# A vision tower's setup: which engine finishes the last parameters, and where the second pictures are waited for

## The reference, cut to what matters

```
y    = relu(batchnorm(conv1_w @ x + conv1_b))          # 64 -> 16 channels
wdyn = conv2_w @ y + conv2_b                           # 9 weights for each place
h    = sum over the 9 taps of shifted(x) * wdyn        # per picture, 64 channels
h    = concat(cls_tok, h)                              # 4 x 4097 x 64
```

```
Lr, Li, Delta = -exp(log_real), imag, exp(log_Delta)
Lbar  = exp(Lr*Delta) * (cos(Li*Delta), sin(Li*Delta))
denom = max(Lr*Lr + Li*Li, 1e-12)
inv_L = (Lr/denom, -Li/denom)
coeff = inv_L * (Lbar - 1)                             # complex product
B_bar = coeff * (B_real, B_imag)
h = h + y_forward + flip(y_backward)      # scan with Lbar, B_bar in, C out, then gelu
```

## Time and profile before

| | us |
|---|---|
| median of three runs | 637.13 |
| lowest and highest of them | 635.39, 638.50 |
| the profiled execution, whole | 637.52 |
| its span, first to last instruction | 636.0 |
| setup, from the span's start to PE's first matmul of the involution | 19.74 |
| involution, from there to PE's first matmul of the next stage | 121.3 |
| PE busy | 567.5 (89%) |
| DVE busy | 504.2 (79%) |
| POOL busy | 423.6 (67%) |
| ACT busy | 291.2 (46%) |

### The profile page before, as it was taken

How to read it: one execution, slowest core, us unless ns; L and a number is a source line. 1 busy time by engine, 2 the same in 40 slices (tenths; PEclk the granted TensorE clock), 3 DMA queues, 4 the chain that set the end, 5 groups by cost and what they waited for, 6 DMA issues and landing times. The chain is left out here.

```text
span 636.0 us, 9633 instructions
## 1 busy us (share of the span) xinstructions
PE 567.5 (89%) x2964; PEld 430.6 (68%) x2964; DVE 504.2 (79%) x919; ACT 291.2 (46%) x822; POOL 423.6 (67%) x641
## 2 busy tenths in 40 slices
PE   0699999985565799999998999999999999999993
PEld 0387878875453688788886667777777777767672
DVE  6688898866663678878789388888888888988885
ACT  3123322225443112235567466766666777655410
POOL 1688999934553033346756178888888888897776
PEclk9999999999785899999999899999999999999998
DMA  6200000000000000000000000000000000000001
GB/s 257 63 3 0 1 2 1 0 0 2 1 1 1 0 1 1 0 1 1 2 1 0 1 1 18 18 17 18 17 19 18 16 18 18 7 11 17 18 18 33
DMA packets 13144, 9.83 MB, mean 15 GB/s; under 512 B 4524, under 2 KB 12844, under 8 KB 12844
## 3 DMA queue, kind: packets, MB, share of 16 engines
q1 hardware_dynamic: 13084, 9.29, 4.6%
q10 hardware_dynamic: 16, 0.00, 0.0%
HBM read 5.10 MB, written 4.20 MB: 15 GB/s over the span
## 5 line engine op out<-in xcount | busy, mean ns | idle before, releaser
L1578 PE MATMUL ex_pE<-ex_WdP,ex_hid 128*128 128x512 f32 (+1 forms) x516 | 183.8, 407 | 0.0
L1578 PEld LDWEIGHTS ex_pE<-ex_WdP,ex_hid 128*128 128x128 f32 (+1 forms) x516 | 96.5, 187 | 32.4 <-issue 11.0
L1821 POOL TENSOR_TENSOR ex_s<-ex_ms 128x1024 f32<-128x1024 f32 (+1 forms) x33 | 83.0, 2514 | 47.4 <-DVE ex_ms L1699 47.2
L1699 DVE TENSOR_TENSOR ex_ms<-ex_pE,ex_gate 128x512 f32<-128x512 f32 x129 | 87.6, 682 | 29.1 <-PE ex_pE L1578 29.0
L1578 PE MATMUL ex_pE<-WdL,ex_hid 128*128 128x512 f32 x258 | 101.7, 394 | 0.0
L816 DVE TENSOR_TENSOR inv_prod<-inv_pW,m_img 128x504 f32<-128x504 f32 x144 | 89.2, 679 | 14.1 <-PE inv_pW L731 13.5
L746 PE MATMUL inv_pS<-ident,inv_prod 128*128 128x128 f32 x576 | 87.3, 275 | 0.7 <-ACT hT L781 0.7
L746 PEld LDWEIGHTS inv_pS<-ident,inv_prod 128*128 128x128 f32 x576 | 71.4, 142 | 16.7 <-DVE inv_prod L816 7.4
L1445 POOL TENSOR_TENSOR hT<-hT,m_M 128x512 f32<-128x512 f32 x24 | 34.0, 1430 | 67.6 <-ACT m_M L1395 67.6
L731 PE MATMUL inv_pW<-inv_ysb,m_conv2L 98*128 98x512 f32 x144 | 75.3, 526 | 2.9 <-DVE inv_ysb L804 2.3
L279 DVE TENSOR_TENSOR ex_hid<-ex_hidf,ex_hid 128x512 fp32r<-128x512 f32 (+1 forms) x64 | 61.1, 973 | 0.0
(11 more groups left out here) (248 smaller groups left out, 1130.7 us busy)
## 6 DMA issues: line engine op xcount, KB each, us to landing
m_img<-in_x SPq DMA_DIRECT2D x2, 2048.0 KB, 9.1
out<-ex_res SPq DMA_DIRECT2D x16, 256.0 KB, 2.3
WdT<-in_L_ffn_Wd SPq DMA_DIRECT2D x2, 256.0 KB
bd<-in_L_ffn_bd SPq DMA_DIRECT2D x16, 2.0 KB
W1d<-in_L_ffn_W SPq DMA_DIRECT2D x2, 64.0 KB
m_Bm<-in_L_attn_fwd_B_real SPq DMA_DIRECT2D x2, 16.0 KB, 1.9
m_Bm<-in_L_attn_fwd_B_imag SPq DMA_DIRECT2D x2, 16.0 KB, 2.1
m_Bm<-in_L_attn_bwd_B_real SPq DMA_DIRECT2D x2, 16.0 KB, 2.0
```

What stands on the lines that cost most here:

```text
L1578: last = nc.tensor.matmul(pE[n % 3][0:P].rearrange("p e f -> p (e f)"), hid[i % 2][value][:, h, par, 128 * j:128 * j + P], WdP[weight][:, ...
L1699: nc.vector.tensor_tensor(ms[b % NB][0:P, t % TPB, :].rearrange("p (e f) -> p e f", e=EX), pE[n % 3][0:P], gate[i % 2][0:P, t, :].unsqueez ...
L1821: nc.gpsimd.tensor_tensor(s4[0:P, 0:T], m[:, :, 0:4 * F], m[:, :, 4 * F:], ALU.add).then_inc(halved, 1)
```

## The change

Five edits, all in the first two stages.

1. DVE's list in setup now ends with the reciprocal (`1/denom`). The fifteen steps on `S` and `decay` that followed leave it.
2. They are written, as sixteen steps, at the head of `state_matrices`, so GpSimd does them at the start of its list in the involution. (One fused step becomes two: a product and a change of sign.) Five of the sixteen are issued without a wait for their own end.
3. The two copies of C (`Cin`, 64 x 64 each) go to GpSimd's list in setup, behind a wait for C's four transfers. PE's transposes of C wait for these copies.
4. The four slices of `m.N` go to ScalarE's list in setup, as activations (`Copy` with a scale), behind a wait for PE's transposes.
5. SP's wait at the end of setup is for the first pictures only. The second pictures have a semaphore of their own, `second_in`, and PE and VectorE wait for it in the involution before they first read them.

The diff, without the lines that only declare a semaphore:

```diff
@@ setup, DVE
                 link(vec.reciprocal(s(15), s(14)))
-                tt(s(16), s(13), s(15), ALU.mult)
-                stt(s(17), imag, -1.0, s(15), ALU.mult, ALU.mult)
-
-                v.wait_ge(c_in, 16 * 4)
-                for d in range(2):
-                    copy(Cin[:, d, 2, :], Cin[:, d, 0, :])
-                count("c_laid")
-                v.wait_ge(exped, 3)
-                v.wait_ge(sined, 3)
-                tt(s(10), s(9), s(9), ALU.mult)
...
-                tt(g.decay[:], s(21), s(21), ALU.mult)
-                v.wait_ge(c_turned, 1)
-                for d in range(2):
-                    ts(m.N[:, 0, d, slot_n(d, 0), :], pC[:, 2 * d, :], sgn[:, 0:1], None, ALU.mult)
-                    ts(m.N[:, 1, d, slot_n(d, 0), :], pC[:, 2 * d + 1, :], -1.0, None, ALU.mult)
@@ setup, SP
-                image(1)
-                sp.wait_ge(img_in, 32)
+                image(1, m.second_in)
+                sp.wait_ge(img_in, 16)
@@ setup, GpSimd
+                pool.wait_ge(c_in, 16 * 4)
+                for d in range(2):
+                    last = nc.gpsimd.tensor_copy(Cin[:, d, 2, :], Cin[:, d, 0, :])
+                last.then_inc(c_laid, 1)
@@ setup, ScalarE
+                act.wait_ge(c_turned, 1)
+                act.wait_ge(dve, consts["sgn"])
+                for d in range(2):
+                    nc.scalar.activation(m.N[:, 0, d, slot_n(d, 0), :], pC[:, 2 * d, :], ACT.Copy, scale=sgn[:, 0:1])
+                    nc.scalar.activation(m.N[:, 1, d, slot_n(d, 0), :], pC[:, 2 * d + 1, :], ACT.Copy, scale=-1.0)
@@ setup, PE
-                pe.wait_ge(dve, consts["c_laid"])
+                pe.wait_ge(c_laid, 1)
@@ state_matrices (GpSimd, in the involution), ahead of all else
+    s = lambda n: S[:, n, :]
+    imag = m.raw[:, 1, :]
+    gp.tensor_tensor(s(16), s(13), s(15), ALU.mult)
+    gp.tensor_tensor(s(17), imag, s(15), ALU.mult)
+    tt(s(10), s(9), s(9), ALU.mult)
+    ts(s(17), s(17), -1.0)
+    ts(s(10), s(10), -2.0, 1.0, ALU.mult, ALU.add)
+    gp.tensor_tensor(s(12), s(4), s(8), ALU.mult)
+    tt(s(11), s(4), s(10), ALU.mult)
+    gp.tensor_tensor(s(20), s(17), s(12), ALU.mult)
+    ts(s(18), s(11), -1.0, None, ALU.add)
+    gp.tensor_tensor(s(21), s(17), s(18), ALU.mult)
+    tt(s(19), s(16), s(18), ALU.mult)
+    tt(s(19), s(19), s(20), ALU.subtract)
+    tt(s(20), s(16), s(12), ALU.mult)
+    tt(s(20), s(20), s(21), ALU.add)
+    tt(s(21), s(4), s(4), ALU.mult)
+    tt(g.decay[:], s(21), s(21), ALU.mult)
@@ involution
+        def starts_second(bp, hc):
+            return bp == 1 and isinstance(hc, int) and hc == 0
@@ involution, PE, reduce
+                    if starts_second(bp, hc):
+                        pe.wait_ge(m.second_in, 16)
@@ involution, DVE, body
+                        if k == 0 and starts_second(bp, hc):
+                            v.wait_ge(m.second_in, 16)
```

More of the change, by code:

```diff
@@ L110, in __init__ @@
         self.b_in = ctx.enter_context(nc.semaphore("b_in"))
+        self.second_in = ctx.enter_context(nc.semaphore("second_in"))
         self.N = sb("N", [128, 2, 2, 5, F])
@@ L342, in setup @@
         ssm_turned = sem("ssm_turned")
-        c_turned = sem("c_turned")
+        c_turned, c_laid = sem("c_turned"), sem("c_laid")
         w_spread = sem("w_spread")
@@ L382, in _ @@
                 fill(sgn[64:128], -1.0)
+                count("sgn")
                 fill(m.M[:, :, :, 5, :], 0.0)
@@ L457, in _, with image @@
                 link(vec.reciprocal(s(15), s(14)))
-                tt(s(16), s(13), s(15), ALU.mult)
-                stt(s(17), imag, -1.0, s(15), ALU.mult, ALU.mult)
-                v.wait_ge(c_in, 16 * 4)
-                for d in range(2):
-                    copy(Cin[:, d, 2, :], Cin[:, d, 0, :])
-                count("c_laid")
-                v.wait_ge(exped, 3)
-                v.wait_ge(sined, 3)
-                tt(s(10), s(9), s(9), ALU.mult)
[L468 to L478, removed]
-                tt(g.decay[:], s(21), s(21), ALU.mult)
-                v.wait_ge(c_turned, 1)
-                for d in range(2):
-                    ts(m.N[:, 0, d, slot_n(d, 0), :], pC[:, 2 * d, :], sgn[:, 0:1], None, ALU.mult)
-                    ts(m.N[:, 1, d, slot_n(d, 0), :], pC[:, 2 * d + 1, :], -1.0, None, ALU.mult)
             @block.sync
             def _(sp):
-                def image(bp):
+                def image(bp, landed):
                     sp.dma_start(img[:, bp, HW:HW + HW * HW],
-                                 g.x[2 * bp:2 * bp + 2].rearrange("b c h w -> (b c) (h w)")).then_inc(img_in, 16)
+                                 g.x[2 * bp:2 * bp + 2].rearrange("b c h w -> (b c) (h w)")).then_inc(landed, 16)
                 sp.dma_start(w1o[:, :], g.conv1_w).then_inc(conv_in, 16)
@@ L495, in _ @@
                     sp.dma_start(bn5[:, n:n + 1], v.rearrange("(p a) -> p a", a=1)).then_inc(conv_in, 16)
-                image(0)
+                image(0, img_in)
                 for d, (_, _, _, _, _, Cr, Ci, _) in enumerate((g.ssm_f, g.ssm_b)):
```

## The result

The changed kernel takes 632.13 us (median of 8 runs, 629.59 to 634.27), the kernel before 637.26 us (8 runs, 633.88 to 638.50). The ratio is 0.9927 with a 95% interval from 0.9910 to 0.9945, so 3.5 to 5.7 us were gained (the medians differ by 5.13 us); the forecast was 3.76 us and 633.4 us, in a range of 631.5 to 636.5.

A forecast was written before the change was run, and what follows sets the result against it. Engines meet at each stage's end, so setup's latest list bounds the involution's first matmul; C's landing, copies, transposes, slices, handovers and meeting put it at 15.98 instead of 19.74 us: 3.76 us less, 637.13 to 633.4 us, range 631.5 to 636.5.

The forecast's parts named there:

- the bounds: Gain at the involution's first matmul with all terms at their ends: from 2.9 to 4.5 us.
- C's landing: Head of the new setup chain: the last of C's four transfers lands at 13.13 us, SP's order being unchanged.
- GpSimd's pair of copies: Setup, after C lands: two 64x64 copies take 0.45 us, ending at 13.68 us.
- PE's four transposes: Setup, after the copies: 0.69 us as before, ending at 14.42 us.
- ScalarE's four slices: Setup, after the transposes: four 128x64 activations take 1.06 us (bounds 0.52 to 1.52), ending at 15.58 us.
- The meeting: End of setup, from the last engine's end to PE's first matmul: 0.40 us, taken between 0.31 and 0.54.
- the two handovers: Setup chain, engine to engine: 0.05 us from GpSimd to PE, 0.10 us from PE to ScalarE.
- Edit 2 costs nothing: Head of GpSimd's involution list: sixteen steps add 3.9 us, GpSimd ends at 132.6 us, 4.4 us of cover remain.
- The waits for the second pictures: In the involution, some 60 us in: cost nothing, as the pictures land at 17.5 us; otherwise all their delay.
- Rival 1: End of setup: engines needing a DMA queue wait behind the second pictures; start 17.9 us, gain 1.8, 635.3 us; chance 0.17.
- Rival 2: Involution's end: GpSimd ends last if its sixteen steps cost over 8.2 us, slower than before from 12.0; chance 0.04.
- Rival 3: Start moves but the involution's ending chain waits elsewhere, or C's copies land later; 637.1 us; chance 0.04.

The follow-up runs named there:

- edit 5 alone: The kernel before, with only the second pictures' own semaphore and their wait moved to the readers; ratio to before 0.9995 (0.9977 to 1.0014).
- edits 3 and 4 undone: The changed kernel with C's copies and the four slices back on VectorE behind the reciprocal; ratio to the kernel before 0.9969 (0.9954 to 0.9985).
- kernel with the longer list: The changed kernel with 28 more unused 128x2 steps behind the sixteen on GpSimd's list; ratio to the kernel before 0.9997 (0.9983 to 1.0012).
- the two kernels that do it: The changed kernel with C's transfers issued by ScalarE, without and with VectorE's list shortened; ratios to the kernel before 0.9990 and 0.9966.
- edit 5 undone: The changed kernel with SP waiting for both pictures at the end of setup again; ratio to the kernel before 0.9983 (0.9964 to 1.0002).

## Why the prediction was right, point by point

The direction, the mechanism and the place were right: the gain is the start, and edits 1 to 5 are worth what the latest list says. The size came out at 4.45 us of start for 3.76, at the upper end of the bounds (4.5). Term by term:

- C's landing was right: the last transfer was issued at 6.63 and GpSimd began at 13.06 us. The handover from a landing took under 0.1 us, and the chain's head came 0.17 us earlier than forecast.
- GpSimd's pair of copies took 0.41 us (0.45 forecast; 0.23 us each). PE's four transposes took 0.68 (0.69).
- ScalarE's four slices took 0.75 us, from 14.25 to 15.00, for 1.06. This is the term that was mis-sized, 0.31 of the 0.69 us. The row of eight that it was taken from has a scale read from memory in each; here every second slice has a constant, takes 0.22 us and lets its successor start after 0.11. The estimate of 0.86 us that the prediction worked out from the Trainium skill ("ScalarE: Activation LUTs", section "What ACT_TABLE_LOAD costs") was the nearer one, since it prices the two kinds apart.
- The meeting took 0.29 us, as in the earlier trace rows (0.31) with ScalarE last, for a middle value of 0.40. Behind VectorE it takes 0.53 to 0.54 in the three profiles where VectorE is last (before, edit 5 alone, edits 3 and 4 undone). There was no reason to go to the middle: the case was known.
- The rest, 0.05 us, are the two handovers, from GpSimd to PE 0.06 us (0.05 forecast) and from PE to ScalarE 0.04 (0.10).
- Edit 2 costs nothing, as forecast: the sixteen steps took 4.4 us (3.9 forecast), and GpSimd ended at 132.08 us (132.6), 3.6 us ahead of ScalarE's last copies (4.4). The kernel with the longer list shows what it costs past the cover.
- The waits for the second pictures cost nothing: the time follows the start. That they would cost as much as the pictures' delay if these came late was not tried.

Rival 1 fell: the engines changed stage between 15.0 and 15.3 us while the second pictures were in flight (issued at 7.27 us, 10.0 us to landing), and the meeting was shorter than before, not longer. From 12 to 16 us the first profile of the changed kernel has packets of the pictures' queue alone (DMA share 0.97) and none of a queue for instructions, so the change of stage, a branch in each list, asked for no code that could have come behind them. That code is fetched hidden beside the work, as the prediction held against this rival, was not tried where a fetch is needed. Rival 2's cause did not occur: the sixteen steps cost 4.4 us and not over 8.2. Its price is borne out: it put the point from which the kernel gains nothing at 12.0 us of added steps, and the kernel with the longer list, whose list on GpSimd took 124.6 us from the start against 112.8 before (11.8 us more), has the time of the kernel before. Rival 3 fell by the table of starts.

## What to carry to other kernels

Where stages end in a meeting of all engines, read each engine's last end and not the busy shares: the longest list gives only its distance to the second longest, and here the shorter list alone moves the start by 1.8 us, the wait moved to the reader alone by nothing, and both together by 4.4 us. Work that leaves the critical list should go to where an engine waits anyway, with that engine's idle time at its stage's end as the budget, and what depends on a late transfer should stand last in its list, or in the next stage. In these runs a small transfer that was needed early had to be issued ahead of a large one; another engine's queue did not help.

## What the runs showed of the hardware that was not expected

- 16 KB transfers landed in 1.9 to 2.2 us when issued ahead of a 2 MB one (from ScalarE's queue, in the two kernels that do it) and in 6.3 to 7.7 us when issued behind it, from SP's queue or ScalarE's.
- The meeting of the engines depends on who is last: 0.29 to 0.31 us behind ScalarE, 0.53 to 0.54 us behind VectorE, about 0.5 us behind SP's wait (edit 5 undone). Why was not tried.
- The first chunk of the involution took from 14.65 to 15.73 us in four executions of one kernel, and what lies behind the involution from 492.0 to 495.1 us, with a granted clock from 0.80 to 0.88 in its first 84 us. Single executions of the kernel before differ by 4 us; which of its stretches make that up was not looked at.
